# Cross-attention: ten of twelve weighted-sum tiles as three rounded products, five of six shifts on VectorE, sums one step later, in straight code

## The reference, cut to what matters

```python
q = rmsnorm((x1 @ Wq).reshape(B, 56, 16, 128), gq)
k = rmsnorm((ctx @ Wk).reshape(B, 1500, 16, 128), gk)
v = (ctx @ Wv).reshape(B, 1500, 16, 128)
attn = softmax(einsum('bqhd,bkhd->bhqk', q, k) / sqrt(128))
out = einsum('bhqk,bkhd->bqhd', attn, v).reshape(B, 56, 2048) @ Wo
```

## Time and profile before

| | us |
|---|---|
| median of 3 runs (1331.40 to 1332.43) | 1332.13 |
| the profiled execution's own time | 1332.16 |
| its span in the profile | 1330.4 |
| TensorE busy | 1307.7 (98%) |
| VectorE busy | 1103.6 (83%) |
| GpSimd busy | 1047.4 (79%) |
| ScalarE busy | 1024.2 (77%) |
| granted TensorE clock, mean share of full | 0.995 |

### The profile page before, as it was taken

One profiled execution on the slowest core, in us unless ns is written; L12 is line 12 of the kernel. 1 busy time (PEld: TensorE's weight loads), 2 busy tenths in 40 slices (PEclk: granted clock), 3 DMA queues, 4 the chain that ended last, 5 costly groups with the idle time before them and its releaser, 6 DMA issues.

```text
span 1330.4 us, 25166 instructions
## 1 busy us (share of the span) xinstructions
PE 1307.7 (98%) x6366; PEld 1034.0 (78%) x6366; DVE 1103.6 (83%) x1715; ACT 1024.2 (77%) x3155; POOL 1047.4 (79%) x968
## 2 busy tenths in 40 slices
PE   8989999999999999999999999999999999999998
PEld 5767677777777777777777777777777777778787
DVE  5866689888888888888888888888888888896675
ACT  2667788888888888888888888888888888873442
POOL 5644442898989898989898988889888989898840
PEclk9989999999999999999999999999999999999999
DMA  7140230000000101010101010101010101030210
GB/s 252 50 156 1 83 131 19 29 17 31 17 32 13 37 12 35 12 36 12 35 12 36 12 35 10 38 8 39 8 40 8 39 8 39 1 111 1 88 50 29
DMA packets 27849, 53.96 MB, mean 41 GB/s; under 512 B 2816, under 2 KB 22400, under 8 KB 25936
## 3 DMA queue, kind: packets, MB, share of 16 engines
q1 hardware_dynamic: 26736, 52.38, 11.7%
q10 hardware_dynamic: 992, 0.36, 0.1%
HBM read 44.60 MB, written 8.13 MB: 40 GB/s over the span
## 4 chain that ended last, share of the span: by engine, by line
PE 92%; DVE 5%; issue 1%; ACT 1%; POOL 1%; DVEq 0%; ACTq 0%
PE xa_k_ps L1376 13%; PE xa_k_ps L1377 13%; PE xa_k_ps L1378 13%; PE xa_o_ps L1465 13%; PE xa_s_ps L1378 6%; PE xa_s_ps L1377 6%; PE xa_s_ps L1376 6%; PE om_ps L1471 3%; PE xa_o_ps L1376 2%; PE xa_o_ps L1377 2%; PE xa_o_ps L1378 2%; PE xq_ps L634 2%; DVE xa_ss L1304 1%; PE xa_o_ps L1393 1%; PE xa_o_ps L1401 1%
## 5 line engine op out<-in xcount | busy, mean ns | idle before, releaser
L1376 PE MATMUL xa_k_ps<-wk_parts,xa_ctxT_hi 128*125 128x512 f32 x768 | 376.5, 490 | 1.2 <-ACT xa_sq L1224 1.0
L1304 DVE TENSOR_REDUCE xa_ss<-xa_sq 125x6 f32<-125x768 f32 x360 | 339.7, 944 | 1.5 <-ACT xa_sq L1224 1.2
L1292 DVE TENSOR_TENSOR xa_scores<-xa_s_ps,xa_rk 125x448 f32<-125x448 f32 x384 | 238.6, 621 | 98.8 <-PE xa_s_ps L1378 97.0
L1377 PE MATMUL xa_k_ps<-wk_parts,xa_ctxT_hi 128*125 128x512 f32 x768 | 303.1, 395 | 0.0
L1378 PE MATMUL xa_k_ps<-wk_parts,ctxT_lo 128*125 128x512 f32 x768 | 302.3, 394 | 0.0
L1135 POOL TENSOR_TENSOR xa_den<-probs,xa_den 125x896 f32<-125x896 f32 x128 | 272.1, 2126 | 3.6 <-ACT probs L1209 3.6
L1209 ACT ACTIVATE probs<-xa_scores 125x896 f32<-125x896 f32 x192 | 183.6, 956 | 102.4 <-DVE xa_scores L1332 37.0
L1189 ACT ACTIVATE xa_sq<-xa_k_ps 125x512 f32<-125x512 f32 x360 | 212.2, 590 | 38.3 <-PE xa_k_ps L1378 21.7
L1223 ACT ACTIVATE xa_k_ps<-xa_k_ps 125x128 f32<-125x128 f32 x720 | 189.1, 263 | 31.2 <-PE xa_k_ps L1378 29.2
L1465 PE MATMUL xa_o_ps<-probs,xa_ctx_nat 125*128 125x448 f32 x448 | 205.4, 539 | 0.0
L1312 DVE TENSOR_TENSOR xa_max_ps<-xa_scores,xa_max_ps 125x448 f32<-125x448 f32 x320 | 198.3, 620 | 0.6
(11 more groups left out here) (186 smaller groups left out, 2360.9 us busy)
## 6 DMA issues: line engine op xcount, KB each, us to landing
xa_ctx_nat<-in_ctx SPq DMA_DIRECT2D x16, 750.0 KB
ctxT_in<-in_ctxT SPq DMA_DIRECT2D x84, 125.0 KB, 2.0
qo<-in_xo_w SPq DMA_DIRECT2D x1, 2048.0 KB, 16.0
qo<-in_xq_w SPq DMA_DIRECT2D x1, 2048.0 KB, 15.6
vo_scratch<-qo SPq DMA_DIRECT2D x2, 1024.0 KB, 4.6
w_parts_scratch<-ws_hi SPq DMA_DIRECT2D x2, 1024.0 KB, 4.1
w_parts_scratch<-ws_lo SPq DMA_DIRECT2D x2, 1024.0 KB, 5.4
...
```

The source lines that it names most:

```text
L1292: dve.tensor_tensor(scores[0:KP, j, :, :], raw, key_scale, ALU.mult).then_inc(s_taken, 1)
L1304: dve.tensor_reduce(ss[:, i // 2, UH * (i % 2):UH * (i % 2) + vector_heads(of)], squares(of, i).rearrange("p (g d) -> p g d", d=XD), AX.X, ...
L1376: pe.matmul(out, l_hi, r_hi, start=first, stop=False)
L1377: pe.matmul(out, l_hi, r_lo, start=False, stop=False)
```

## The change

- each_phase has no loop any more; all 18 groups are straight code, and every wait is against a constant.
- PAIR_SPLITS makes tiles 2 to 11 of a half three products (10 of 12); LAST_SPLITS keeps the old five for batch 15. p_hi holds both tiles of a pair, and ScalarE writes it and GpSimd takes its low part for 896 columns where both are split.
- The rounded natural-layout context (nat_hi) covers ten tiles, in one buffer and three parts: ScalarE makes parts of 256, 256 and 768 columns at steps 17, 17 and 21 of a group, GpSimd the remainders at 18, 18 and 23 (before: 256 columns at 8 and 384 at 12).
- VECTOR_SHIFTS: VectorE shifts five of six pairs, at steps 2, 3, 5, 7 and 8 (before three, at 2, 4 and 6); GpSimd shifts one, at step 0 of the next half (before three). Each has a semaphore of its own.
- PV_LAG is 21 instead of 20, TD 9 instead of 8: a half's weighted sum begins at step 9, which is also the step of its predecessor's denominators.
- The ring of scores has 20 places instead of 24, to make room.

```diff
-def each_phase(eng, body, loop_end):
-
-    for b in (-1, 0, 1):
-        body(Phase(b))
-    with eng.Fori(1, loop_end // 2) as pair:
-        for i in range(2):
-            body(Phase(None, pair, i))
-    for b in range(loop_end, B + 1):
+def each_phase(body):
+
+    for b in range(-1, B + 1):
         body(Phase(b))
...
-PV_LAG = EXP_LAG + 5
+PV_LAG = EXP_LAG + 6
 LOW_LAG = EXP_LAG + 3
-NAT_SPLITS = (8, 12)
-TD = 8
+TD = 9
...
+EARLY_STEPS = 18
...
+VECTOR_SHIFTS = {2: 0, 3: 2, 5: 4, 7: 6, 8: 8}
+VS, GS = 5, 1
...
 def vector_shifts(y):
-    return y % KT < KT // 2
+    return y % KT < 2 * VS
...
+PAIR_SPLITS = (0, 2, 2, 2, 2, 2)
+SPLIT_TILES = [2 * i + o for i, n in enumerate(PAIR_SPLITS) for o in range(2 - n, 2)]
+LAST_SPLITS = (0, 1, 1, 1, 1, 1)
+NAT_PARTS = slice(2, 4), slice(4, 6), slice(6, 12)
+LAST_PARTS = slice(3, 6, 2), slice(7, 8), slice(9, 12, 2)
+NAT_ENDS = 4, 6, KT
...
+NAT_HI_AT = {17: (0, 1), 21: (2,)}
+NAT_LO_AT = {18: (0, 1), 23: (2,)}
+SC = 20
...
-        nat_hi = sb("xa_nat_hi", [KP, 2, SPLIT_PAIRS, C], F32R)
-        p_hi = sb("xa_p_hi", [KP, NPR // 2, UW], F32R)
+        nat_hi = sb("xa_nat_hi", [KP, len(SPLIT_TILES), C], F32R)
+        p_hi = sb("xa_p_hi", [KP, NPR // 2, 2, UW], F32R)
-        scores = sb("xa_scores", [P, STEPS, UH, T])
+        scores = sb("xa_scores", [P, SC, UH, T])
...
-                        pool.tensor_tensor(probs_r[0:KP, (y + 1) % NPR, :], probs[0:KP, (y + 1) % NPR, :],
-                                           p_hi[:, y // 2 % (NPR // 2), :].bitcast(F32), ALU.subtract
+                        first = 2 - split_tiles(ph, y)
+                        slots = slice(y % NPR + first, y % NPR + 2)
+                        pool.tensor_tensor(probs_r[0:KP, slots, :], probs[0:KP, slots, :],
+                                           p_hi[:, y // 2 % (NPR // 2), first:2, :].bitcast(F32), ALU.subtract
                                            ).then_inc(p_lo_ready, 1)
...
-                        if y % KT:
-                            act.activation(p_hi[:, y // 2 % (NPR // 2), :], score_slot(y + 1), ACT.Exp
+                        if split_tiles(ph, y) == 2:
+                            act.activation(p_hi[:, y // 2 % (NPR // 2), :, :], score_pair(ph, y), ACT.Exp
                                            ).then_inc(p_hi_ready, 1)
...
+                    if ph.within(0, 15):
+                        for part in NAT_HI_AT.get(j, ()):
+                            act.wait_ge(nat_loaded[ph.parity()], nat_loads(ph))
+                            wait(act, pv_done, ph.at(STEPS, NAT_ENDS[part] - KT))
+                            act.activation(nat_hi_part(ph, part), nat_part(ctx_nat, ph, part), ACT.Copy).then_inc(nat_hi_ready, 1)
...
-                        wait(dve, exp_done, ph.at(STEPS, j - STEPS + 1))
-                        dve.tensor_tensor(scores[0:KP, j, :, :], raw, key_scale, ALU.mult).then_inc(s_taken, 1)
+                        wait(dve, exp_done, ph.at(STEPS, j - SC + 1))
+                        wait(dve, p_hi_ready, pairs_split(ph, j - SC))
+                        dve.tensor_tensor(scores[0:KP, ph.at(STEPS, j) % SC, :, :], raw, key_scale, ALU.mult
+                                          ).then_inc(s_taken, 1)
...
-                    y = lagged_pair(ph, j, SHIFT_LAG)
-                    pairs = [y] if y is not None and vector_shifts(y) else []
+                    pairs = [KT * (h - 1) + VECTOR_SHIFTS[t]] if t in VECTOR_SHIFTS and ended_half(ph, h) else []
...
                         if ty == 0:
-                            pe.wait_ge(shift_done, ph.at(STEPS, y + (KT if ph.b == B else KT // 2)))
+                            pe.wait_ge(vector_shifted, vector_shifts_done(ph, y + KT - 2))
...
-                        if ty % 2 and ty > 1:
-                            pe.wait_ge(p_lo_ready, pairs_split(ph, y - 1))
+                        if ty % 2 >= 2 - split_tiles(ph, y):
+                            pe.wait_ge(p_lo_ready, pairs_split(ph, y))
```

More of the change, by code:

```diff
@@ L869, in adds_done, with vector_shifts_done, pool_shifts_done, tiles_of @@
     return ph.at(2 * ADDS, ADDS * half + max(k, 1))
+VECTOR_SHIFTS = {2: 0, 3: 2, 5: 4, 7: 6, 8: 8}
+VS, GS = 5, 1
 def vector_shifts(y):
-    return y % KT < KT // 2
+    return y % KT < 2 * VS
+def vector_shifts_done(ph, y):
+    last = ph.b + y // STEPS == B - 1 and y // KT % 2
+    return ph.at(2 * VS, VS * (y // KT) + (y % KT // 2 + 1 if last else min(y % KT // 2 + 1, VS)))
+def pool_shifts_done(ph, y):
+    return ph.at(2 * GS, GS * (y // KT) + y % KT // 2 + 1 - VS)
+PAIR_SPLITS = (0, 2, 2, 2, 2, 2)
[4 more added lines that the diff above has]
+NAT_ENDS = 4, 6, KT
+def tiles_of(part):
+    return list(range(KT))[part]
+def split_tiles(ph, y):
+    return (LAST_SPLITS if ph.b + y // STEPS == B - 1 else PAIR_SPLITS)[y % KT // 2]
+def nat_parts(ph):
+    return LAST_PARTS if ph.b == B - 1 else NAT_PARTS
+def nat_place(ph, tile):
+    return [t for part in nat_parts(ph) for t in tiles_of(part)].index(tile)
+NAT_HI_AT = {17: (0, 1), 21: (2,)}
+NAT_LO_AT = {18: (0, 1), 23: (2,)}
+SC = 20
 SPLIT_PAIRS = KT // 2 - 1
@@ L891, in early_products @@
         first, last = 3 * (j - 4), 3 * (j - 3)
-    elif ph.b == B and j < STEPS - TD + 2:
+    elif ph.b == B and j < EARLY_STEPS:
         first, last = 3 * (STEPS - 4) + 2 * j, 3 * (STEPS - 4) + 2 * (j + 1)
@@ L969, in spread_pair, with nat_part, nat_hi_part @@
             return o_ps[0:KP, (y // KT) % 2, 0:UW].unsqueeze(1).broadcast_to([KP, 2, UW])
-        def odd_tiles(nat, ph, part):
-            first, last = ODD_PARTS[part]
-            return nat[:, ph.parity(), :, :].rearrange("p (t o) c -> p t o c", o=2)[:, first:last, 1, :]
-        def odd_hi(ph, part):
-            first, last = ODD_PARTS[part]
-            return nat_hi[:, ph.parity(), first - 1:last - 1, :]
+        def nat_part(nat, ph, part):
+            return nat[:, ph.parity(), nat_parts(ph)[part], :]
+        def nat_hi_part(ph, part):
+            tiles = tiles_of(nat_parts(ph)[part])
+            at = nat_place(ph, tiles[0])
+            return nat_hi[:, at:at + len(tiles), :]
         def probs_pair(y):
@@ L1063, in _ @@
             mlp.load_raw(sp)
-            each_phase(sp, body, 12)
+            each_phase(body)
             mlp.sync_tail(sp)
@@ L1146, in body @@
                         pool.wait_ge(den_done, adds_done(ph, y))
[L1147 to L1148 removed]
+                        first = 2 - split_tiles(ph, y)
+                        slots = slice(y % NPR + first, y % NPR + 2)
+                        pool.tensor_tensor(probs_r[0:KP, slots, :], probs[0:KP, slots, :],
+                                           p_hi[:, y // 2 % (NPR // 2), first:2, :].bitcast(F32), ALU.subtract
                                            ).then_inc(p_lo_ready, 1)
[L1150 to L1154 removed]
+                    if ph.within(0, 15):
+                        for part in NAT_LO_AT.get(j, ()):
+                            pool.wait_ge(nat_hi_ready, ph.at(len(NAT_PARTS), part + 1))
+                            pool.tensor_tensor(nat_part(nat_r, ph, part), nat_part(ctx_nat, ph, part),
+                                               nat_hi_part(ph, part).bitcast(F32), ALU.subtract).then_inc(nat_lo_ready, 1)
                     if t == 6 and ph.within(0, 15) and not (ph.b == 15 and h == 1):
                         q_low(ph.shift(h), 1 - h)
[L1158 removed]
+            each_phase(body)
             mlp.gpsimd_tail(pool, pv_done)
@@ L1204, in body @@
                     if y is not None:
-                        wait(act, shift_done, ph.at(STEPS, y + 2))
+                        if vector_shifts(y) or ph.b == B and y >= -KT:
+                            act.wait_ge(vector_shifted, vector_shifts_done(ph, y))
+                        else:
+                            act.wait_ge(pool_shifted, pool_shifts_done(ph, y))
                         wait(act, pv_done, ph.at(STEPS, y - NPR + 2))
@@ L1456, in body @@
                                 pe.wait_ge(nat_loaded[of.parity()], nat_loads(of))
-                                pe.wait_ge(nat_lo_ready, of.at(2, 2))
-                        if ty % 2 and ty > 1:
-                            pe.wait_ge(p_lo_ready, pairs_split(ph, y - 1))
-                            three(o_ps[:, hy, 0:UW], nat_hi[:, of.parity(), ty // 2 - 1, :],
-                                  nat_r[:, of.parity(), ty, :], p_hi[:, (y - 1) // 2 % (NPR // 2), :],
+                        for part, tiles in enumerate(nat_parts(of)):
+                            if hy == 0 and ty == tiles.start:
+                                pe.wait_ge(nat_lo_ready, of.at(len(NAT_PARTS), part + 1))
+                        if ty % 2 >= 2 - split_tiles(ph, y):
+                            pe.wait_ge(p_lo_ready, pairs_split(ph, y))
+                            three(o_ps[:, hy, 0:UW], nat_hi[:, nat_place(of, ty), :],
+                                  nat_r[:, of.parity(), ty, :], p_hi[:, y // 2 % (NPR // 2), ty % 2, :],
```

65 lines of the change are left out of this document (28 added, 37 removed).

## The result

| | before | after |
|---|---|---|
| median of 4 runs, us | 1331.87 (1331.4 to 1332.43) | 1323.51 (1322.9 to 1323.89) |
| ratio, 95% interval | | 0.9937 (0.9925 to 0.995) |
| span of the profiled execution, us | 1330.4 | 1321.1 |

The change makes the kernel 8.4 us faster by the medians, 9.3 by the spans of the two profiled executions; the forecast was 7 us (1325.1).

What follows compares the result with a forecast made beforehand. The prediction took TensorE's own work to bound the kernel. Its terms, -21 + 7 + 2 + 3 + 2 = -7 us from 1332.16, gave 1325.1 us, range 1318 to 1331 (1312 to 1339 with rivals).

Steps and rivals of the forecast that it cites:

- What bounds: Kernel before: TensorE's own work bounds it, 67.35 us a batch; other engines each have some 8 us to spare.
- The gain: TensorE: each tile converted to three products takes 0.14 us less; 150 tiles in batches 0 to 14, -21 us.
- A: Step 9: ScalarE's second square delays step 11's key product 0.5 us in 14 second halves, not first halves: +7 us.
- T: The start of step 9 on TensorE, from which the prediction counts times within a half.
- B: Steps 7 and 8: VectorE's fifth shift delays the first plain sum 0 to 0.12 us, 30 times; taken as +2.
- C: Entry into group 15: GpSimd's low parts come late for TensorE; between 0 and +4 us, taken as +3.
- D: First halves of group 0: two more shifts, five wider roundings on ScalarE and VectorE; 0 to +4 us, taken as +2.
- Nothing for the rest: Score ring, places of exponentials, GpSimd's low part, context load and longer lag's tail: taken as no cost.
- The ring of 20: Score ring of 20 places: five steps of cover (14 us), so no cost.
- the loop: Back edges: VectorE's 2.04 us idle, six times, is covered by slack, so straight code counts 0.
- the first: Rival: the waits of ScalarE in step 9 and VectorE in steps 7 and 8 are covered; 1316 us, chance 0.22.
- The fifth: Rival: VectorE and GpSimd exclude each other on 60 added shifts; 60 us on VectorE, some 1360 us, chance 0.02.

Runs made afterwards that it cites:

- The runs at ten tiles and two edits: The changed kernel with ScalarE's last context rounding in step 22 instead of 21 (1316.6 us), then with the first four tiles' roundings one step later too (1315.22 us).
- the run with the rounding moved: The changed kernel with ScalarE's rounding of the last six context tiles in step 22 instead of 21: 1316.6 us.
- the old lag: The changed kernel with weighted sums and the closing of the denominators back in their old step (PV_LAG 20, TD 8): 1434.08 us.
- the old tiles in the new frame: The changed kernel with the old choice of tiles (five as three products, seven plain) and 448-column low parts in every group: 1333.44 us.

## Why the prediction was right, by its steps

**What bounds.** TensorE did, and each us off its stream counted until another engine was late at one instruction. The runs at ten tiles and two edits show TensorE busy for 65.70 of 65.7 us.

**The gain**, 0.14 us per tile, 21 us: groups 1 to 14 hold 140 of the 150 converted tiles and lose 942.16 - 921.96 = 20.20 us where nothing waits, 0.144 each; 21.6 for all. The step worked from two neighbouring rows and was right to a hundredth.

**A**, 0.5 us in 14 second halves, nothing in first halves, +7: the step is 3.30 us in second halves and 2.76 in first, 0.54 x 14 = 7.6, and moving one instruction took 7.85 us out of these groups. First halves: ScalarE's second square ends at 738.12 and the key product starts at 738.17, with no wait marked. The mechanism was right; that the size came out so near is in part luck, because the due time was wrong. The working let the product start at T + 6.0 when nothing is late, where first halves have 738.17 - 732.54 = 5.63 and the run with the rounding moved 701.76 - 696.11 = 5.65: two whole steps count the 0.35 us that a plain product leaves in the record behind it, and that lies after the start. Two things balanced it. The product follows the square's end within 0.05 us, where 0.2 was allowed for the weight load. And a late product takes less: it starts 705.38 - 699.00 - 5.63 = 0.75 us late, but the next record only 0.57 (705.71 against 738.68, each less its T). That ScalarE's end (T + 6.35) came out at T + 6.33 is because its terms were starts to starts of the same instructions (from the closing on 4.35 us, measured 4.41, behind a start 0.08 too late).

**B**, between 0 and +4, taken as +2: it was 0. VectorE's fifth shift,

```profile
700.12 1.08 DVE L1375 TENSOR_TENSOR xa_scores<-xa_scores,xa_o_ps 125x896 f32<-125x896 f32 x1
```

ends at 701.20, T + 2.2 instead of T + 2.3, and the first plain sum starts at 701.43 without a wait. The prediction's terms don't give its T + 2.3 either: 1.6 + 0.2 + 0.2, and 0.1 from the shift's last start to the end of its record, are T + 2.1, before the T + 2.3 at which it wanted the weight load. With its own sum it could have booked nothing. The step that holds it takes 3.17 us, against 3.16 before. The margin is real though small: the old lag costs 2.3 us a half plus the clock.

**C**, between 0 and +4, taken as +3: group 15 takes 1.12 us more, where the 9 converted tiles whose sums fall into it should have made it 1.3 shorter: C is 2.4. The first four steps don't shrink to 1.3 us each, as the working had it: they take 6.73 us together, and took 6.74 before. One of the waits is

```profile
1185.21 0.47 PE L1419 MATMUL xa_o_ps<-xa_p_hi,xa_nat_hi 125*128 125x448 f32 x1 [1.12 <-POOL probs_r L1184]
```

TensorE's records there mark 1.6 us more of waits than before: this 1.12, 0.36 for the load of vo, and 0.56 against 0.42 for VectorE. Another 0.5 is at a second low part, in step 7, where only the weight load bears a mark and the step takes 2.89 us against 2.53 before, though its tile is converted:

```profile
1190.61 0.19 PEld L1419 LDWEIGHTS xa_o_ps<-xa_p_hi,xa_nat_hi 125*128 125x128 f32 x1 [0.48 <-POOL probs_r L1184]
```

Where the last 0.3 sits stays open. Of the waits expected in the first six steps only one was for a low part.

**D**, between 0 and +4, taken as +2: group 0 takes 1.65 us more though one sum (0.7, the tail's) has left it and one tile (0.1) is converted: 2.5. The earlier trace rows had 3.5 us of weight-load waits there. The place was right: TensorE's records have waits of 1.95 us for ScalarE's square, 1.03 before, and of 1.00 for VectorE's shift, which is new. Of the two causes that the working named only one acted: the old tiles in the new frame have 2.3 of the 2.5, so the moved shifts and the lag make D, and the five wider roundings, booked at 2.0 us of ScalarE's time, make 0.2. Shifts and lag were not separated there.

**Nothing for the rest**: the tail is longer by the moved sum alone, 0.70, which group 0 has less. The ring of 20, the 8 places of exponentials and the loop show no row of TensorE's, and the old tiles in the new frame are 1.4 us above the kernel before, with 2.3 of D among it: nothing is left for the rest.

**Sum.** -21.6 + 7.6 + 0 + 2.4 + 2.5 = -9.1; with -0.42 before the first score product, and 0.25 that groups 1 to 14 take more than gain and A make, it is the -9.3 of the spans. Of the 2.1 us between -7 and -9.1, B is 2.0; the gain (0.6) and A (0.6) were each off in opposite ways, and so were C (0.6) and D (0.5). That these two pairs cancel is luck; with B at nothing, the forecast would have been 1323.1. Of the rivals the first needed A to be covered: it took an edit to reach its 1316 us. The fifth, VectorE and GpSimd shutting each other out, would have shown as long shifts: this one takes 1.08 us beside a low part of GpSimd's that started at 700.13.
